# A post-norm attention and FFN kernel: the FFN down product taken part by part of its sum, and GpSimd's centring of x placed behind the second norm

## What is computed

```python
def _layernorm(x, axis=-1, eps=1e-05):
    m = jnp.mean(x, axis=axis, keepdims=True)
    v = jnp.var(x, axis=axis, keepdims=True)
    return (x - m) / jnp.sqrt(v + eps)

# attention, 12 layers, 16 heads of 8 channels, no softmax
    att = jnp.einsum('bhqd,bhkd->bhqk', q, k) * scale
    y = jnp.einsum('bhqk,bhkd->bhqd', att, v)
    x = y @ Wproj[i].T + bproj[i] + x
# ffn
    gate = jnp.einsum('bsd,hd->bsh', x, wg)
    up = jnp.einsum('bsd,hd->bsh', x, wu)
    h = jax.nn.silu(gate) * up
    return jnp.einsum('bsh,dh->bsd', h, wd)
# whole
    x = _layernorm(x + attn(x));  x = _layernorm(x + ffn(x))
```

## Time and profile before

| | us |
|---|---|
| median of 3 runs (lowest, highest) | 336.1 (335.86, 336.31) |
| the profiled execution's own time | 335.32 |
| its span, from the first to the last record | 333.5 |
| TensorE matmul busy | 317.8 (95% of the span) |
| VectorE busy | 226.4 (68%) |
| ScalarE busy | 183.0 (55%) |
| GpSimd busy | 96.6 (29%) |
| layers, up to the last product of layer 12 | about 258 |
| chunks 0 to 7, from the first gate matmul to the end | 271.63 to 333.5 |

### The profile page before, as it was taken

How to read it: one execution, slowest core, us unless ns; L and a number is a source line. 1 busy time by engine, 2 the same in 40 slices (tenths; PEclk the granted TensorE clock), 3 DMA queues, 4 the chain that set the end, 5 groups by cost and what they waited for, 6 DMA issues and landing times.

```text
span 333.5 us, 8348 instructions
## 1 busy us (share of the span) xinstructions
PE 317.8 (95%) x3336; PEld 288.9 (87%) x3336; DVE 226.4 (68%) x638; ACT 183.0 (55%) x417; POOL 96.6 (29%) x89
## 2 busy tenths in 40 slices
PE   8899999999999999999999999999999999999993
PEld 7879889798897998979979799797997988888873
DVE  1167676775775757757677576676765569998974
ACT  3338757376483774846738467385572164444550
POOL 2006046050320502305023050140505034555533
PEclk9999999999999999999999999999999999999999
DMA  8751001010010200102002010020000000111112
GB/s 232 267 220 61 4 2 61 2 63 2 2 61 3 63 0 3 63 0 63 2 2 62 2 52 12 2 62 2 2 3 2 0 1 0 31 48 46 33 34 67
DMA packets 10660, 13.66 MB, mean 41 GB/s; under 512 B 512, under 2 KB 8832, under 8 KB 10496
## 3 DMA queue, kind: packets, MB, share of 16 engines
q1 hardware_dynamic: 8368, 11.94, 11.4%
q10 hardware_dynamic: 2256, 1.21, 1.3%
HBM read 11.04 MB, written 2.10 MB: 39 GB/s over the span
## 4 chain that ended last, share of the span: by engine, by line
PE 80%; DVE 9%; issue 3%; DMA 3%; ACT 2%; POOL 1%; ACTq 0%; POOLq 0%; DVEq 0%
PE ps L797 14%; PE ps L850 13%; PE ps L885 13%; PE ps L748 6%; PE ps L746 6%; PE ps L747 6%; PE ps L964 3%; PE ps L806 3%; PE ps L836 3%; DMA xt<-x_tok 3%; DVE s_rows L581 3%; PE ps L813 2%; DVE xt L681 2%; DVE mt L574 2%; PE ps L953 1%
## 5 line engine op out<-in xcount | busy, mean ns | idle before, releaser
L346 POOL TENSOR_TENSOR step_lo<-step,step_hi 128x512 fp32r<-128x512 f32 x44 | 54.9, 1279 | 180.3 <-ACT step_hi L430 180.3
L746 PE MATMUL ps<-state_hi,step_hi 128*128 128x258 f32 x176 | 50.7, 288 | 0.0
L850 PE MATMUL ps<-s_rows,w 32*128 32x256 f32 x768 | 44.8, 380 | 5.5 <-DVE s_rows L581 5.5
L748 PE MATMUL ps<-state_hi,step_lo 128*128 128x258 f32 x176 | 49.9, 283 | 0.0
L747 PE MATMUL ps<-state_lo,step_hi 128*128 128x258 f32 x176 | 49.6, 282 | 0.0
L850 PEld LDWEIGHTS ps<-s_rows,w 32*128 32x128 f32 x768 | 40.4, 185 | 7.4 <-ACT s_rows L424 7.4
L430 ACT CAST step_hi<-step 128x512 fp32r<-128x512 f32 x44 | 27.0, 619 | 33.8 <-DVE step L586 33.8
L797 PE MATMUL ps<-w,gram 128*128 128x128 f32 x352 | 44.0, 278 | 0.0
L797 PEld LDWEIGHTS ps<-w,gram 128*128 128x128 f32 x352 | 41.1, 192 | 1.0
L885 PE MATMUL ps<-step,gram 128*128 128x128 f32 x320 | 40.6, 281 | 0.0
L885 PEld LDWEIGHTS ps<-step,gram 128*128 128x128 f32 x320 | 37.3, 192 | 3.3 <-DVE step L586 3.3
(11 more groups left out here) (103 smaller groups left out, 502.7 us busy)
## 6 DMA issues: line engine op xcount, KB each, us to landing
w<-weights SPq DMA_DIRECT2D x12, 496.5 KB, 3.5
xchan<-x_chan SPq DMA_DIRECT2D x1, 2048.0 KB, 10.6
out<-xchan SPq DMA_DIRECT2D x7, 256.0 KB, 2.4
xt<-x_tok ACTq DMA_DIRECT2D x4, 256.0 KB, 7.5
xt<-x_tok SPq DMA_DIRECT2D x4, 256.0 KB, 5.3
fw_int<-ffn_weights SPq DMA_DIRECT2D x1, 576.0 KB, 4.8
out<-xchan SPq DMA_DIRECT2D x2, 128.0 KB, 2.4
cst<-consts ACTq DMA_DIRECT2D x1, 154.5 KB, 4.4
```

The source lines that it names most:

```text
L346: nc.gpsimd.tensor_tensor(group(step_lo, g), group(step, g), group(step_hi_f, g), ALU.subtract).then_inc(step_lo_ready, 1)
L746: nc.tensor.matmul(dst, l_hi, r_hi, start=True, stop=False)
L748: return nc.tensor.matmul(dst, l_lo, r_hi, start=False, stop=True)
L850: last = nc.tensor.matmul(n_banks(h)[:, k, :], w[r, s, WQ + P * i:WQ + P * (i + 1)], s_rows[r, h, i, :], start=i == 0, stop=i == QUADS - 1)
```

## The change

In GpSimd's `chunk` the centring of chunk c+3 moves from ahead of norm2 c to behind it. In TensorE's `down_stage` the loops over t and j change places: for each part j there is one wait for `hid_ready`, and then the matmuls of all four groups t. The matmul that opens a bank (`start`) is now only the first one into that bank, the other groups' first matmuls have `start` off and land on columns that this opening has cleared. The number of matmuls is the same.

```diff
                 if ahead >= 2:
                     pool.wait_ge(h1_ready, (c + 1) * CT + CT)
                     rstd1_part(c + 2)
+                if ahead > 0:
+                    norm2(c)
                 if ahead >= 3:
                     pool.wait_ge(z_done, c + 2)
                     centre(c + 3, 1 - slot)
-                if ahead > 0:
-                    norm2(c)
...
             def down_stage(n, last_chunk=False):
                 pe.wait_ge(y_ready, n + 1)
-                for t in range(CT):
-                    for j in range(HC):
-                        if t == 0:
-                            pe.wait_ge(hid_ready, n * HC + (HC + j + 1))
+
+                first, final = ((0, CT // 2), (CT // 2 - 1, CT - 1)) if last_chunk else ((0,), (CT - 1,))
+                for j in range(HC):
+                    pe.wait_ge(hid_ready, n * HC + (HC + j + 1))
+                    for t in range(CT):
                         bank = HT_BANK if last_chunk and t >= CT // 2 else DOWN_BANK
                         last = nc.tensor.matmul(ps[:, bank, P * t:P * (t + 1)], hid[:, j, P * t:P * (t + 1)],
-                                                wd[:, j, :], start=j == 0, stop=j == HC - 1)
-                    if last_chunk and t == CT // 2 - 1:
-                        last.then_inc(down_done, 1)
+                                                wd[:, j, :], start=j == 0 and t in first, stop=j == HC - 1 and t in final)
+                        if last_chunk and j == HC - 1 and t == CT // 2 - 1:
+                            last.then_inc(down_done, 1)
                 last.then_inc(down_done, 1)
```

## The result

| | us |
|---|---|
| before, median (lowest, highest) | 336.2 (335.9, 336.3) |
| changed, median of 4 runs (lowest, highest) | 350.8 (347.9, 352.4) |
| ratio, 95% interval | 1.043 (1.036 to 1.050) |
| the changed kernel's profiled execution, its span | 352.37, 350.5 |

The changed kernel is slower by 14.7 us. The forecast was 345.2 with a range of 344.0 to 347.5: the side is right, the size is not, and the measured time lies outside the range. The unusual thing in the table is the spread: 4.5 us between the four runs, where the kernel before spreads over 0.4. The run of 347.9 also has the highest mean granted clock of the four, 0.988 against 0.973 to 0.977. In all that follows two executions far outside the rest, one of 633.0 us (the kernel with the centring between) and one of 799.4 us (the kernel before), both at a clock of 1.00, are left out.

The account below looks back on a forecast made before the run. TensorE was taken to bound the kernel, 80% of the chain of waits. Late centring +9.9, chunk 6 -0.83 and chunk 7 +0.04 gave +9.1 us: 344.4 profiled, 345.2 as median, range 344.0 to 347.5.

Parts of the forecast that it names:

- G+2.26, 4.51, 5.55 and 5.70: Times from a chunk's first gate weight load (G): norm2's power starts, its product ends, centring ends, z stage loads.
- The period without the clock: Chunks 1 to 5: z stage's load at 5.70, plus 0.94 to the down stage, plus 2.68 for it: 9.32 us.
- +9.9: Chunks 1 to 5: the late centring makes five periods of 9.32, 46.6 us instead of 36.71.
- the sum: Whole kernel: 9.9 - 0.83 + 0.04 = +9.1 us, taking the profiled 335.32 to 344.4.
- what the forecast added to get from the profiled execution to the median: Whole kernel: the profiled execution lies 0.8 us below the median of 336.1, so 344.4 becomes 345.2.
- Chunk 6 and chunk 7: Down stage by parts: chunk 6 takes 5.92 instead of 6.75, -0.83 us; chunk 7's first half comes 0.20 later, +0.04.
- the rival of the falling clock: TensorE's clock falls because it idles 2.46 us in each of five chunks: 379 or 362 us; chance 3%.
- a share of 34 us: Half the clock for all work of five chunks: up to 34 us more, 379; for half of them 362.
- The alternation of groups in the bank: Down stage: each matmul takes its whole load of 0.19 instead of 0.112, 1.9 us in eight chunks, 360; chance 2%.
- more than 2.7 us: Sign that the forecast is wrong: 24 records of a down stage take more than 2.7 us.
- The centring in time: Centring ends before G+3.1 and the z stage doesn't wait: periods of 6.86 in chunks 1 to 5, 332.9; chance 2%.
- The 0.83 us of VectorE: VectorE's third square of y, beside the centring, takes 1.12 us instead of 0.29; the 0.83 comes back each time.

Follow-up runs that it names:

- the kernel with the centring between: The changed kernel with the centring between norm2's power and its product, so 1.2 us earlier: 338.0 us, ratio 1.005.
- the filled kernel: The changed kernel with ten unread products of a zero tile ahead of the z stage's wait for the centring: 345.97 us, ratio 1.030.
- one-chunk-ahead version: The changed kernel, but GpSimd centres chunk c+4 instead of c+3 behind norm2 c, chunk 3 ahead of the loop: 332.1 us, ratio 0.988.
- the fourth kernel: Centring one chunk further ahead than the changed kernel, but chunk 7's centring alone left late, behind norm2 of chunk 4: 336.0 us, ratio 0.999.
- centring alone: The kernel before with only the centring moved behind norm2: 350.0 us, ratio 1.041.
- the one-chunk-ahead kernel with the old down stage: The changed kernel centring c+4 instead of c+3, with the down stage as before (t outside, j inside): 333.3 us, ratio 0.991.

## Why the prediction was right or wrong

**What bounds the kernel, and the wait.** Right. The centring has a reader 0.79 us behind it, and norm2's wait puts it 2.3 us too late. The steps read G+2.26, 4.51, 5.55 and 5.70 in the forecast; chunk 1 after has G+2.26, 4.50, 5.50 and 5.65. The period without the clock was forecast at 9.32 and is 9.20. Of that 0.12, 0.05 is the centring's end and 0.05 the way from the z stage to the down stage: 0.89 in chunk 1 after, where I took the 0.94 of chunk 2 before. With five chunks this part was +9.9 in the sum and measured +9.2. Without the falls, then, the kernel takes 343.7 by the median, 1.5 below the forecast and 0.3 below its range: 0.7 is the period, and 0.8 is what the forecast added to get from the profiled execution to the median, of which the filled kernel shows nothing (its profiled execution is its median, 345.97).

**Chunk 6 and chunk 7.** -0.83 forecast, -0.84 measured. In chunk 7 the first half of y comes 0.22 us later (344.30, from 338.86, against the earlier trace rows), as worked out (0.20). The second half comes 0.04 earlier (345.38), where 0.04 later was forecast, and the stretch to the end grew by 0.03 all the same. That its size agrees with the forecast 0.04 is luck: the step that was to give it went the other way, and what did give it isn't shown.

**The clock.** This is the step that failed. The sum took each wait of 2.46 us to cost its own length and put the clock behind it at nothing; in the profile four of the five cost 1.63 us more each, 6.5 us in all. I gave the rival of the falling clock 3%, because behind the last matmul the clock stays 1.00 for over 4 us, and the new gaps last 2.46. That compared two different things. The clock's fall comes late, and it comes whether or not TensorE is at work again by then: at 287.4 in chunk 1 the idle stretch had been over since 286.17, and in all ten falls of the three profiles TensorE was at work again, for 0.06 to 1.3 us. A record that still shows 1.00 after 4 us of rest says nothing about a rest of 2.4 us that is followed by work, because its fall is then booked on the work. A row that could have told was missing from the trace of before. Its longest idle stretch of weight loads between work is one of the transfers at the start:

```profile
11.13 2.75 PEld L765 LDWEIGHTS ps<-xt 128*128 128x128 f32 x24 [1.18 <-DMA xt<-x_tok]
```

The right use of it is a bound: nothing above 1.2 us was shown to be safe. With the rule of the Trainium skill that I had cited (TensorE: Matmul & The Clock Gate, "What's actually happening": default throttled, released by activity), that should have moved a large part of the chance, and the upper end of the range, to this rival. Its price was mis-sized as well: not a share of 34 us, but 1.63 us a fall, since the clock comes back within the chunk. Four falls on top of the 343.7 measured without them give 350.2, and the median is 350.8.

**Other rivals.** The alternation of groups in the bank costs nothing: 24 loads took 2.76 us wherever the clock was 1.00 and nothing was waited for, as before. (The sign named for this, "more than 2.7 us", was set too low: the 2.76 of the earlier trace rows would already have met it. The 2.68 of the sum runs to the next gate load, the 2.76 to the end of the last.) The centring in time, the rival on the other side, was worked out at 332.9. The one-chunk-ahead version makes it true, and it took 332.1.

**What the change was to gain.** The 0.83 us of VectorE did come back, as worked out. The Trainium skill's exclusive lock (SBUF — State Buffer, "SBUF: two separate sides") agrees here too. The groups of chunks 1 to 5 show it, after and then before (line, engine, operation, count | busy us, mean ns | idle us): twenty squares of y take 4.6 us instead of 8.8, and five centrings 5.2 instead of 5.8. GpSimd's product and centring now lie beside VectorE operations with one input in PSUM and hold none of them up. After:

```profile
L327 POOL TENSOR_TENSOR xc<-xchan,neg_mu 128x512 f32 (+1 forms) x5 | 5.2, 1038 | 0.0
L664 DVE CUSTOM_DVE_ANT_0 sq<-y 128x128 f32<-128x128 f32 x20 | 4.6, 288 | 0.2
```

Before:

```profile
L664 DVE CUSTOM_DVE_ANT_0 sq<-y 128x128 f32<-128x128 f32 x20 | 8.8, 495 | 0.2
L327 POOL TENSOR_TENSOR xc<-xchan,neg_mu 128x512 f32 (+1 forms) x5 | 5.8, 1167 | 0.0
```

## What to carry to other kernels

Before a step is moved behind a wait, find its reader and the slack between them; if the step must go there, let it serve one round further ahead, which here turned a loss of 14.7 us into a gain of 4.1. An idle stretch of TensorE costs its length and, at 2.25 us and more in ten of thirteen cases here, also a fall of the clock that is booked on the matmuls behind it: look at the granted clock there, and test by filling the stretch with unread products. When the trace shows no idle stretch of the length that a change will make, the clock is an unknown and belongs in the range.

## What the runs showed of the hardware

- Idle stretches of 1.09 to 1.89 us in five periods running never cost the clock in three profiles, and neither did one of 1.50 us at the start of the fourth kernel. Of the stretches of 2.25 to 2.45 us that a profile shows, ten of thirteen did (changed kernel 5 of 6, centring alone 4 of 5, one late centring 1 of 1, the start of the one-chunk-ahead kernel with the old down stage 0 of 1).
- The granted clock fell to half 0.06 to 1.3 us after TensorE had begun again, at another distance in almost every chunk, and was back some 3.4 us later.
- With the centring (1.19 us) beside them, one of four squares takes 1.12 us instead of 0.29, and the others keep their length.
- The changed kernel's four runs differ by 4.5 us, where the kernel before spreads over 0.4 us beside them and over 1.0 to 2.4 us beside the experiments. The spread was a sign of falls whose number differs from run to run; the mean granted clock of each run is the better one (0.973 to 0.988 here, 0.994 to 1.000 for the kernel before, beside the experiments).
